# Reciprocal roots of the query and key lengths: from ScalarE's root and VectorE's reciprocal to GpSimd's addition and power

## The reference

```python
def rmsnorm(x):
    return x * jax.lax.rsqrt(jnp.mean(x * x, axis=-1, keepdims=True) + RMS_EPS)
...
q = (x @ Wq.T).reshape(B, T, 2 * H, hd)      # 16 short heads of 8 numbers
k = (x @ Wk.T).reshape(B, T, 2 * H, hd)
v = (x @ Wv.T).reshape(B, T, H, 2 * hd)
q = apply_rotary(rmsnorm(q), cos, sin)
k = apply_rotary(rmsnorm(k), cos, sin)
```

## Time and profile before

| | us |
|---|---|
| median of 3 runs | 752.62 |
| lowest and highest run | 749.7, 755.53 |
| the profiled execution's own time | 751.81 |
| its span, first to last instruction | 750.1 |
| of it the projection phase | 0 to 109.9 |

### The profile page before, as it was taken

The page is one execution under the profiler, slowest core; times in us unless marked ns, Lnnn a source line. Parts: engine busy times, 40 slices in busy tenths (PEclk is TensorE's granted clock), DMA queues, the critical chain, the costliest instruction groups (busy, mean ns, idle before and its releaser), DMA issues. The chain is left out here.

```text
span 750.1 us, 15925 instructions
## 1 busy us (share of the span) xinstructions
PE 613.8 (82%) x4811; PEld 366.4 (49%) x4812; DVE 520.5 (69%) x1444; ACT 498.2 (66%) x844; POOL 325.3 (43%) x479
## 2 busy tenths in 40 slices
PE   6677757999999999999999979876784587888870
PEld 5455542333333333333333348656563586877860
DVE  4899776889797978888888769864653343434475
ACT  2388776989899999899998962432333344656651
POOL 0334443344444434343434434253645355554551
PEclk9799897999999999999999998987976899999995
DMA  7000000006655555556666005111202122222285
GB/s 186 29 28 29 14 33 25 1 3 107 106 99 98 89 99 92 87 75 105 106 106 107 1 2 196 43 38 57 77 27 61 43 72 61 79 71 65 79 240 154
DMA packets 76266, 56.06 MB, mean 75 GB/s; under 512 B 6528, under 2 KB 70848, under 8 KB 75968
## 3 DMA queue, kind: packets, MB, share of 16 engines
q1 hardware_dynamic: 70688, 46.01, 29.4%
q0 software_dynamic: 4352, 8.99, 3.5%
q10 hardware_dynamic: 1184, 0.56, 0.3%
HBM read 15.36 MB, written 28.65 MB: 59 GB/s over the span
## 5 line engine op out<-in xcount | busy, mean ns | idle before, releaser
L814 ACT ACTIVATE attend_prob<-attend_ring 128x1024 f32<-128x1024 f32 (+1 forms) x320 | 280.1, 951 | 16.7 <-PE attend_ring L960 14.7
L758 POOL TENSOR_SCALAR_AFFINE_SELECT attend_prob<-attend_prob 128x256 f32<-128x256 f32 x256 | 118.5, 486 | 141.7 <-ACT attend_prob L814 140.4
L980 PE MATMUL attend_ps_o<-attend_prob,attend_v_slot 128*32 128x512 f32 (+3 forms) x1536 | 157.2, 497 | 0.0
L1933 POOL DMA_INDIRECT expert_outputs<-routed_linear_gated,routed_expert_goal_now x72 | 70.6, 980 | 71.8 <-DVE routed_linear_gated L1977 57.8
L1060 POOL DMA_INDIRECT slots<-rows,slot_index x64 | 62.1, 970 | 66.1 <-issue 37.0
L960 PE MATMUL attend_ring<-attend_qk_slot 32*128 32x512 f16 (+3 forms) x672 | 80.1, 329 | 8.1 <-ACT attend_prob L814 6.3
L960 PEld LDWEIGHTS attend_ring<-attend_qk_slot 32*128 32x128 f16 x672 | 22.4, 91 | 106.7 <-ACT attend_prob L814 37.6
L1954 DVE TENSOR_TENSOR outed_linear_head_normed<-outed_linear_head_normed,routed_linear_ps_c 128x256 f32<-128x256 f32 x72 | 30.2, 420 | 43.7 <-ACT outed_linear_head_normed L2047 31.2
L2047 ACT ACTIVATE outed_linear_head_normed<-routed_linear_ps_c 128x256 f32<-128x256 f32 x72 | 27.5, 382 | 46.0 <-PE routed_linear_ps_c L2094 33.0
L2094 PE MATMUL routed_linear_ps_c<-outed_linear_head_normed,head_turned 128*128 128x128 f32 x384 | 53.4, 284 | 4.5 <-ACT outed_linear_head_normed L2023 3.4
L980 PEld LDWEIGHTS attend_ps_o<-attend_prob,attend_v_slot 128*32 128x32 f32 x1536 | 33.7, 108 | 45.0 <-issue 37.8
(11 more groups left out here) (294 smaller groups left out, 1276.6 us busy)
## 6 DMA issues: line engine op xcount, KB each, us to landing
slots<-attend_zeros SPq DMA_DIRECT2D x24, 715.0 KB, 10.6
attend_qk_slot<-qk_parts SPq DMA_DIRECT2D x14, 512.0 KB, 3.1
x_pairs<-slots SPq DMA_DIRECT2D x72, 65.0 KB
v_all<-expert_outputs SPq DMA_DIRECT2D x8, 512.0 KB, 4.4
xn_all<-project_xn SPq DMA_DIRECT2D x8, 256.0 KB, 2.3
w<-w_laid SPq DMA_DIRECT2D x1, 2048.0 KB, 7.7
rows<-rows SPq DMA_DIRECT2D x4, 512.0 KB
out<-xn_all SPq DMA_DIRECT2D x8, 256.0 KB, 3.1
```

Of the source, the lines that this page charges most:

```text
L758: ins = nc.gpsimd.affine_select(out=edge, in_=edge, compare_op=ALU.is_ge, fill=0.0, base=0, pattern=[[0, 2], [1, P]], channel_multiplier=-1)
L814: nc.scalar.activation(probs(k, pair)[:, :, 0:width], scores[:, :, 0:width], ACT.Exp, scale=HD ** -0.5).then_inc(exp_made[u][pair], 1)
L980: ins = nc.tensor.matmul(ps_o[RB * s:RB * (s + 1), off:QC], v4[slot][:, j, s], probs(k, s // 2)[:, s % 2, at:at + cols], start=j == 0, sto ...
L1933: pool.indirect_dma_start(m.outputs, bass.IndirectOffsetOnAxis(goal_now[i][:, j:j + 1], 0), y_out[i][:, j * P:(j + 1) * P], None).then_inc ...
```

## The change

The squares are scaled so that their sum over a head is the mean. GpSimd then adds a tensor that holds the guard everywhere and raises the result to a tensor that holds -0.5 everywhere, both 128x128, at the start of its body for group `c`, ahead of the products. ScalarE's root and VectorE's reciprocal are gone. GpSimd waits for `summed`, its addition signals `msq_made`, and VectorE's next sum waits for that before it overwrites the sums.

```diff
@@ VectorE, body
                     dve.wait_ge(squared, 2 * g + 2)
+                    once(dve, msq_made, g)
                     nc.vector.tensor_reduce(ssum, sq.rearrange("p (n d) -> p n d", d=HD), AX.X, ALU.add).then_inc(summed, 1)
...
                     add_halves(b)
-                    dve.wait_ge(rooted, g + 1)
-                    once(dve, unit_made[1], g)
-                    nc.vector.reciprocal(rrms, sroot).then_inc(rrms_made, 1)
@@ GpSimd, body
                 if c:
                     g, odd = c
+                    pool.wait_ge(summed, g + 1)
+                    once(pool, unit_made[1], g)
+                    nc.gpsimd.tensor_tensor(msq, ssum, guard, ALU.add).then_inc(msq_made, 1)
+                    pool.wait_ge(msq_made, g + 1)
+                    nc.gpsimd.tensor_tensor(rrms, msq, minus_half, ALU.pow).then_inc(rrms_made, 1)
                     pool.wait_ge(rrms_made, g + 1)
...
+            nc.gpsimd.memset(guard, RMS_EPS)
+            nc.gpsimd.memset(minus_half, -0.5)
             nc.gpsimd.memset(m.ident, 0.0).then_inc(const_made, 1)
@@ ScalarE, square and body
                 nc.scalar.activation(sq.rearrange("p (t c) -> p t c", t=GT)[:, tiles], qkv4[:, tiles, 0:2 * C],
-                                     ACT.Square).then_inc(squared, 1)
+                                     ACT.Square, scale=HD ** -0.5).then_inc(squared, 1)
...
-                if b:
-                    g, odd = b
-                    act.wait_ge(summed, g + 1)
-                    nc.scalar.activation(sroot, ssum, ACT.Sqrt, bias=m.eps_rms[:, 0:1], scale=1.0 / HD).then_inc(rooted, 1)
```

## The result

| | before | after |
|---|---|---|
| median of 4 runs | 754.08 us (749.7 to 756.18) | 873.09 us (870.75 to 876.79) |
| profiled execution, its span | 751.81, 750.1 us | 873.01, 871.2 us |
| end of the projection phase | 109.87 us | 235.62 us |
| one turn of the loop | 9.48 us | 26.17 us |
| mean granted clock | 0.92 | 0.86 |

The ratio is 1.159, with the interval 1.152 to 1.166: 119 us slower. The forecast was 777 with 800 as the upper end. The direction was right and the size was not. All of it lies in the phase that the change touches: the phase ends 125.7 us later, and the rest takes 4.6 us less than before (635.6 against 640.2).

A forecast was written before the change was run, and what follows sets the result against it. It took the ring through `xn`, TensorE, ScalarE and GpSimd's L401, with shared access in turns, as the bound. Loop +21.0, first turn +2.6 and end +1.5 gave +25.1 on 751.81: 777 us, range 751 to 800.

The forecast's parts named there:

- The price of the power: New 128x128 power on GpSimd, one per group: taken as 3.2 us, lower bound 0.3, upper bound 6.
- The price of the addition: New 128x128 addition on GpSimd, one per group: taken as 0.3 us, from 2.2 ns per element of a partition.
- Any GpSimd instruction keeps VectorE out for its whole length: Projection phase: GpSimd instructions and VectorE's `xn`, copies, rotations and FP4 steps exclude each other whole, taking turns.
- the fourth `xn` is late by S: Loop: addition and power get in between the four `xn`, delaying the last and the next turn; 6 x 3.5 = +21.0.
- S: GpSimd's added time per group, addition plus power: 0.3 + 3.2 = 3.5 us; total loss 8S - 2.9.
- B: Theory set against the forecast's in the experiments: the power leaves the shared access free; the loss is GpSimd's own chain.
- the ring: Projection loop: `xn` waits for L401, that for ScalarE's L450 and L452, these for the matmul, that for `xn`; turn 9.48 us.
- the dear power: Rival: power of 6 us or more on GpSimd, turns taken; +47.5, 799.3 us, 811 at the lower clock; chance 0.15.
- The removed work at 0: Loop: dropping VectorE's reciprocal (0.94 us) and ScalarE's root (0.41) only becomes idle time; the turn stays.
- the -0.9 of the first turn: First turn: cos starts with no wait for ScalarE, so there the removed reciprocal saves 0.9 us.
- The clock: TensorE's clock may fall in the loop: +11.8 us with all four higher-level turns low; left to the range.
- The signs named: Powers of 2 to 5 us, four `xn` near 5, turn near 13, longer VectorE and ScalarE waits, L395 right behind rotations.

The follow-up runs named there:

- e3: Kernel before plus an added stretch behind the projection groups timing powers and additions on GpSimd, alone and beside VectorE; its 128x128 power took 21.6 us (base 50), 20.8 (base 1).
- e7: Changed kernel with the power on 24 of the 128 elements and a product on the other 104: 755.22 us against 750.37, ratio 1.0063.
- e1: Changed kernel with a product in place of the power, reciprocal root left out: 683.58 us against 681.67 for the kernel before, ratio 1.0028.
- e2: Kernel before without VectorE's reciprocal, GpSimd multiplying by ScalarE's scaled root: 681.54 us against 681.67, ratio 1.0003.
- e6: Kernel before with ScalarE's reciprocal root in one activation replacing root and reciprocal, for lengths and rows' deviation: 680.32 us against 681.67, ratio 0.9975.
- e10: Kernel before with e6's edit and ScalarE's rounding of the queries (L450) moved ahead of the second square: 742.53 us against 751.91, ratio 0.9856.
- e8: Changed kernel with the power on 64 of the 128 elements and a product on the other 64: 797.74 us against 751.91, ratio 1.0613.
- before_again: Second profile of the unchanged kernel before, taken with the second set of runs: projection phase ends at 111.65 us, the rest takes 636.0.

## Why the forecast was right in direction and wrong in size

- **The price of the power: failed.** 3.2 us with an upper bound of 6; it is 21.05 (in the changed kernel and in e3). The bound was the step that failed: "both functions as ten simple passes each". It went by VectorE's reciprocal, a row of another engine. No row of the kernel before showed GpSimd at a function of this kind, so nothing bounded it from above, and the text should have said so instead of ending the price at 6. This is the first of two steps that failed.
- **The price of the addition: mis-sized.** 0.3 taken; 0.45 to 0.50 measured. The 2.2 ns an element came from the distance between starts of 128x512 instructions, and a short one pays a part that doesn't shrink. What `xn` saw of it is less, not more: about 0.22 (e7's +0.22, half of e1's +0.45).
- **"Any GpSimd instruction keeps VectorE out for its whole length": the second step, failed for the power.** For GpSimd's products and differences of 128x512 it nearly stands: L269 at 95.17 takes 0.95 more and ends only when L405, which lasts to 96.24, has. For 128x128 it does not: `xn` grows by 0.45 for e1's two instructions of 0.46 together, L271 by 0.26 beside an addition of 0.50, e3's twelve by 0.14 for each addition. The power holds the access for 0.26, half a power for 0.13. All but e3's fit roughly one estimate from these rows, 2 ns an element (1.0 for 512, 0.26 for 128, 0.13 for 64), for the power as for the others; why e3's additions cost less was not followed, and no run was made to test the estimate. The Trainium skill, "SBUF — State Buffer", section "Who interferes with whom", says that whoever issues first gets the shared pair for the whole instruction. The rows of L405 nearly agree with it, those of L392 (four `xn` in 1.12 inside it) do not, and the measurement decides. So the step "the fourth `xn` is late by S" didn't happen: S = 21.5 would have given 8 x 21.5 - 2.9 = +169 and 921 us, and the kernel takes 873. What stood in its place is GpSimd's own chain, 21.05 + 5.1 = 26.2 a turn.
- **The two errors pulled opposite ways.** By B, with the 3.2 us of the forecast, GpSimd's chain would be 3.2 + 5.1 = 8.3, under the ring's 9.9 (e1), and the change would cost the few us of e1 to e7, within 1% (an estimate; no run has a power of 3.2). So of the forecast's +25, the mechanism's part would not have come. That the direction came true is luck: it was saved by the power being more than six times dearer than thought.
- **The rival that came nearest** was the dear power, by its name only: its 799 to 811 still had 6 us and the wrong mechanism. That GpSimd itself fills the turn was no rival, and should have been one: the earlier trace rows gave its chain, L395 twice, L398, L401 at 4.3 us in starts, so that with the addition (0.5) and a short wait for L450 it is about 5 (5.1 measured), and any power over 9.48 - 5.1 = 4.4 us makes it the longest.
- **The removed work at 0: right.** e2 gives 0.9983 to 1.0024 for the reciprocal; that has room for the -0.9 of the first turn, but doesn't show it. The root's zero agrees with e6 and e1, but no run took the root alone away.
- **The ring through `xn`: right as long as GpSimd's chain is the shorter one.** e1's +0.45 of `xn` came back as +0.44 of the turn, and e10, which takes GpSimd out of `xn`'s way, shortens it to 9.26. With a power of 10.8 us (e8) `xn` grows to 3.54 and the turn does not follow it.
- **The clock: not separable.** TensorE was granted 0.67 to 0.74 in the three windows shown, where the kernel before has 1.00 from 60 to 80, but it has its work done 10 us before the power ends, so the lower level costs nothing in the loop.
- **The signs named.** VectorE's wait before cos is larger (2.46 against 0.22) and ScalarE waits longer (15.53): these came. `xn` near 5 us did not (1.12), the turn near 13 is 26.17, and L399 comes 20 us behind the rotations instead of right behind them. The first pointed to B; the other two show the length of the power.

## What to carry to other kernels

Before a function moves to an engine that no row shows doing it, measure that one instruction at two sizes; if it can't be measured, leave the range open above instead of bounding it by another engine's rows. Then add up the receiving engine's own chain for one turn with the new work in it: half busy means only that the new work may take the other half, here about 4.4 us. And removing work from the busiest engine gains nothing where its branch is the shorter one (e2); the version furthest under the kernel before moved one activation of the ring earlier (e10, 1.4%), and not all of that gain was traced.

## What the runs showed of the hardware that was not expected

- GpSimd's power of two tensors takes 21.05 us for 128x128, 10.6 to 10.8 for 128x64, 4.17 for 128x24 and 2.9 for 128x16, whatever the base; its addition of 128x128 takes 0.45 to 0.50. ScalarE's reciprocal root of 128x128 takes 0.42.
- A long instruction on GpSimd need not hold the access that it shares with VectorE: 0.26 us in the first 13 of 21 here, 0.13 for half the elements. An addition or product of 128x128 held it for 0.22 to 0.26 of its 0.46 to 0.50. One of 128x512 held up a copy for nearly its whole length (1.23 instead of 0.28 beside L405). Additions can get in between VectorE instructions that follow one another without a gap (3.77 instead of 3.2 for twelve beside four additions), which the forecast had left open.
- The same kernel takes 681.67 us on one chip and 750 to 752 on two others, with the same turn in the projection phase (9.48 in e2 and e6 on the first, 9.48 in `before_again` on the second), so the 70 us lie mostly behind that phase (behind it e6's profile has 571.5 us, `before_again` 636.0). Why was not looked into.
